# Self-attention with the keys on partitions: scores made turned, maxima from a rough first pass, totals by a ones matmul

## What is computed

```python
def cross_attention(x, ctx, wq, wk, wv, wo, bo):      # self-attention: x and ctx are both layer_norm(x)
    q = jnp.einsum('bne,ef->bnf', x, wq).reshape(B, N, HEADS, DHEAD).transpose(0, 2, 1, 3)
    k = jnp.einsum('bme,ef->bmf', ctx, wk).reshape(B, M, HEADS, DHEAD).transpose(0, 2, 1, 3)
    v = jnp.einsum('bme,ef->bmf', ctx, wv).reshape(B, M, HEADS, DHEAD).transpose(0, 2, 1, 3)
    scores = jnp.einsum('bhnd,bhmd->bhnm', q, k) * SCALE
    attn = jax.nn.softmax(scores, axis=-1)
    out = jnp.einsum('bhnm,bhmd->bhnd', attn, v)
    out = out.transpose(0, 2, 1, 3).reshape(B, N, HEADS * DHEAD)
    return jnp.einsum('bnf,fe->bne', out, wo) + bo
```

## Time and profile before

| | us |
|---|---|
| median of 3 runs | 1040.16 (1039.8 to 1040.65) |
| span of the profiled execution | 1036.7 |
| TensorE busy in it | 981.3 |
| VectorE busy | 690.3 |
| ScalarE busy | 591.5 |
| GpSimd busy | 380.1 |

### The profile page before, as it was taken

How to read it: one execution, slowest core, us unless ns; L and a number is a source line. 1 busy time by engine, 2 the same in 40 slices (tenths; PEclk the granted TensorE clock), 3 DMA queues, 4 the chain that set the end, 5 groups by cost and what they waited for, 6 DMA issues and landing times.

```text
span 1036.7 us, 17534 instructions
## 1 busy us (share of the span) xinstructions
PE 981.3 (95%) x6376; PEld 707.1 (68%) x6376; DVE 690.3 (67%) x1171; ACT 591.5 (57%) x1332; POOL 380.1 (37%) x493
## 2 busy tenths in 40 slices
PE   7999978999999999999999999999989999999998
PEld 4566666666667656667666667666647589999887
DVE  2767646677773776773676773776753889999563
ACT  2666634766763667763667763667753555455442
POOL 2576623434332344342344341343330024444220
PEclk9999999999999999999999999999999999999999
DMA  6400050000000000000000000000000340000000
GB/s 134 94 2 1 1 147 1 1 1 2 1 1 2 1 1 2 1 1 1 2 1 1 1 1 1 2 1 1 2 1 8 101 110 1 1 1 1 2 26 26
DMA packets 25370, 17.64 MB, mean 17 GB/s; under 512 B 8565, under 2 KB 24101, under 8 KB 25285
## 3 DMA queue, kind: packets, MB, share of 16 engines
q1 hardware_dynamic: 25285, 16.52, 6.6%
HBM read 11.26 MB, written 1.31 MB: 12 GB/s over the span
## 4 chain that ended last, share of the span: by engine, by line
PE 64%; DVE 10%; ACT 5%; issue 4%; POOL 1%; DMA 0%; SPq 0%; DVEq 0%; ACTq 0%; POOLq 0%
PE banks L409 13%; PE banks L396 12%; PE banks L382 11%; PE banks L416 4%; ACT sa_probs L499 3%; PE banks L224 3%; PE banks L227 2%; PE banks L226 2%; PE banks L225 2%; PE banks L1641 2%; PE banks L1933 2%; DVE sa_negmax L571 2%; DVE ca_top L1776 2%; DVE ca_probs L1781 1%; PE banks L232 1%
## 5 line engine op out<-in xcount | busy, mean ns | idle before, releaser
L639 POOL TENSOR_SCALAR sa_probs<-sa_probs,sa_inverse 128x512 f32<-128x512 f32 x320 | 217.7, 696 | 372.4 <-DVE sa_inverse L575 372.3
L499 ACT ACTIVATE sa_probs<-banks,sa_negmax 128x512 f32<-128x512 f32 x320 | 215.8, 685 | 163.5 <-DVE sa_negmax L571 163.4
L571 DVE TENSOR_REDUCE sa_negmax<-banks 128x2 f32<-128x1024 f32 x160 | 188.8, 1219 | 12.4 <-PE banks L382 9.7
L396 PEld LDWEIGHTS banks<-ident,sa_probs 128*128 128x128 f32 x1280 | 145.7, 141 | 55.6 <-issue 27.6
L396 PE MATMUL banks<-ident,sa_probs 128*128 128x128 f32 x1280 | 174.0, 277 | 10.0 <-ACT sa_turned L510 5.8
L580 DVE COPY sa_turned<-banks 128x512 f32<-128x512 f32 x160 | 110.2, 689 | 76.3 <-PE banks L396 76.3
L409 PE MATMUL banks<-sa_turned,sa_v 128*64 128x512 f32 x640 | 155.0, 605 | 0.0
L382 PE MATMUL banks<-sa_k_parts,sa_q_parts 64*128 64x512 f32 x960 | 134.9, 412 | 1.9 <-ACT sa_probs L499 1.9
L510 ACT COPY sa_turned<-banks 128x512 f32<-128x512 f32 x160 | 94.3, 590 | 30.6 <-PE banks L396 28.8
L382 PEld LDWEIGHTS banks<-sa_k_parts,sa_q_parts 64*128 64x128 f32 x960 | 85.2, 187 | 31.2 <-issue 14.4
L409 PEld LDWEIGHTS banks<-sa_turned,sa_v 128*64 128x64 f32 x640 | 38.7, 136 | 74.3 <-issue 73.0
(11 more groups left out here) (218 smaller groups left out, 1724.9 us busy)
## 6 DMA issues: line engine op xcount, KB each, us to landing
w_o<-in_L_xattn_wo SPq DMA_DIRECT2D x2, 800.0 KB, 9.2
out<-x SPq DMA_DIRECT2D x4, 320.0 KB, 2.4
w_q_t<-in_L_xattn_wq_t SPq DMA_DIRECT2D x1, 1120.0 KB, 10.4
fold_values<-ca_turned SPq DMA_DIRECT2D x5, 192.5 KB
x<-in_x SPq DMA_DIRECT2D x1, 960.0 KB, 5.8
fold_values<-ca_probs SPq DMA_DIRECT2D x4, 192.5 KB
w_q_t<-in_L_xattn_wq SPq DMA_DIRECT2D x1, 640.0 KB, 6.6
w_o<-in_L_xattn_wk SPq DMA_DIRECT2D x1, 640.0 KB, 10.0
```

Of the source, the lines that this page charges most:

```text
L396: last = pe.transpose(b_turn[e][:, q * P:(q + 1) * P], probs[:, j % 2, e, q, k * P:(k + 1) * P], ident[:])
L499: act.activation(probs[:, j % 2, e, q, :], b_scores[u % 2][:, e, :], ACT.Exp, bias=negmax[:, u % RING, e:e + 1], accum_out=total[:, u % RI ...
L571: dve.tensor_reduce(negmax[:, u % RING, :], b_scores[u % 2], AX_X, ALU.max, negate=True).then_inc(s_max.sem, 1)
L639: pool.tensor_scalar(probs[:, j % 2, e, q, :], probs[:, j % 2, e, q, :], inverse[:, u % RING, e:e + 1], 1.0, ALU.mult, ALU.mult).then_inc( ...
```

## The change

The loop now runs over 40 pairs g = 10 b + j. The scores are made with the keys on partitions (k the stationary operand, q the moving one), so the exponentials come out in the form in which the product with v wants them, and the transposes and their copies are gone. The maximum over keys can't be taken along partitions, so it comes from a first pass: `rough_scores` makes hi·hi alone with queries on partitions, VectorE takes the negated maxima into `negmax` (columns 0 and 64 of 65, the rest zero), `turn_shift` turns them into a row for each head, ScalarE copies the rows into `shift`, and each unit of `scores` gets a fourth product, ones times `shift`, which subtracts the maximum. (Any shift near the maximum gives the same softmax.) ScalarE makes one exponential of 128 x 1024 a unit, without bias or total. GpSimd adds the four units' probabilities (`add`, three additions of 128 x 1024); `totals` multiplies the sum by ones, which spreads each query's total over 64 partitions; VectorE inverts that in four pieces of 128 columns (`invert`), and multiplies `att` by it (`normalize`), after the product with v. The copy of v moves from VectorE to ScalarE. `project_out` works in column halves, and for the first three batches it stands inside the pair with j = 1 of the next batch; so the operands of the norm are doubled (`ln.second`). GpSimd fills the constants at the start. The scores of unit k of a pair, the rough scores of the next pair and the products of the pair ahead alternate in TensorE's order.

```diff

...
-    NU = NPAIR * QT
-    ND = NU // 2
-    LEAD = 2
-    RING = 8
+    NG = B * NPAIR
+    NK = S // P
+    RING = 3
+    V_RING = 2
+    PIECES = 4
+    STATS_AT, HAT_AT, TURN_MAIN, TURN_TAIL, ROUND_AT = 2, 3, 4, 5, 6
...
-        probs = sb("probs", [P, 2, 2, QT, S])
-        turned = sb("turned", [P, 2, 2, S])
+        q_parts = sb("q_parts", [P, RING, 2, S], F32R)
+        k_parts = sb("k_parts", [P, RING, 2, S], F32R)
+        v = sb("v", [P, V_RING, QT, 2 * P])
+        probs = sb("probs", [P, NK, 2, S])
+        sums = sb("sums", [P, 2, 2, S])
         att = sb("att", [P, NPAIR, S])
+        negmax = sb("negmax", [P, 2, QT, HD + 1], F32R)
+        shift = sb("shift", [P, 2, S], F32R)
+        inverse = sb("inverse", [P, S])
+        ones_r = sb("ones_r", [P, P], F32R)
+        ones = sb("ones", [P, HD])
+        ident_r = sb("ident_r", [P, P], F32R)
+        ln.second = (sb("y_hi", [P, S], F32R), sb("y_lo", [P, S], F32R), sb("y_tail", [3 * DT, S], F32R))
...
-        b_scores, b_turn, b_out, b_proj = [banks.pair(0), banks.pair(2)], banks[4:6], banks[6], banks[7]
+        b_keys, b_max = [banks.pair(0), banks.pair(2)], banks.pair(4)
+        b_proj, b_v, b_shift, b_out, b_sum = banks[0], banks[1], banks[4], banks[6], banks[7]
...
+            def rough_scores(g, u, bank):
+                if u == 0:
+                    pe.wait_ge(s_qhi.sem, s_qhi.at(0, g))
+                    pe.wait_ge(s_khi.sem, s_khi.at(0, g))
+                for e in range(2):
+                    last = pe.matmul(bank[:, e, :], q_parts[half(e), g % RING, 0, u * P:(u + 1) * P], k_parts[half(e), g % RING, 0, :],
+                                     start=True, stop=True)
+                last.then_inc(s_rough.sem, 1)
+
+            def next_rough(g, u):
+                pe.wait_ge(s_max.sem, s_max.at(0, unit(g, u) - 1))
+                if u == 0:
+                    pe.wait_ge(s_shift.sem, s_shift.at(0, g - 1))
+                rough_scores(g, u, b_max)
+
+            def turn_shift(g):
+                if g == 0:
+                    pe.wait_ge(s_ident, 1)
+                pe.wait_ge(s_max.sem, s_max.at(0, unit(g, QT - 1)))
+                for i in range(QT):
+                    last = pe.matmul(b_shift[0:HD + 1, i * P:(i + 1) * P], negmax[:, g % 2, i, :], ident_r[:], start=True, stop=True)
+                last.then_inc(s_row.sem, 1)
+
+            def scores(g, k):
+                if k == 0:
+                    pe.wait_ge(s_qlo.sem, s_qlo.at(0, g))
+                    pe.wait_ge(s_klo.sem, s_klo.at(0, min(g + 1, NG - 1)))
+                    pe.wait_ge(s_vsb.sem, s_vsb.at(0, min(g + 1, NG - 1)))
+                    pe.wait_ge(s_shift.sem, s_shift.at(0, g))
...
+                if unit(g, k) >= 2:
+                    pe.wait_ge(s_exp.sem, s_exp.at(0, unit(g, k) - 2))
+                bank = b_keys[k % 2]
+                for i, (a, c) in enumerate(((0, 0), (0, 1), (1, 0))):
                     for e in range(2):
+                        pe.matmul(bank[:, e, :], k_parts[half(e), g % RING, a, k * P:(k + 1) * P], q_parts[half(e), g % RING, c, :],
+                                  start=(i == 0), stop=False)
+                for e in range(2):
+                    last = pe.matmul(bank[:, e, :], ones_r[half(e), :], shift[half(e), g % 2, :], start=False, stop=True)
...
-            def turns(b, u):
-            def pv(b, u):
+            def products(g, k):
+                pe.wait_ge(s_exp.sem, s_exp.at(0, unit(g, k)))
                 if k == 0:
+                    pe.wait_ge(s_vsb.sem, s_vsb.at(0, g | 1))
+                    if g > 0:
+                        pe.wait_ge(s_raw.sem, s_raw.at(0, g - 1))
                 for e in range(2):
+                    c = g % 2 * P + e * HD
+                    last = pe.matmul(b_out[half(e), :], v[:, g // 2 % V_RING, k, c:c + HD], probs[:, k, e, :],
+                                     start=(k == 0), stop=(k == NK - 1))
+                last.then_inc(s_pv.sem, 1)
+
+            def totals(g):
+                pe.wait_ge(s_add.sem, s_add.at(0, (NK - 1) * g + NK - 2))
+                if g > 0:
+                    pe.wait_ge(s_inv.sem, s_inv.at(0, PIECES * g - 1))
+                for e in range(2):
+                    last = pe.matmul(b_sum[half(e), :], ones[:], sums[:, g % 2, e, :], start=True, stop=True)
+                last.then_inc(s_sum.sem, 1)
+
+            def project_out(bank, q, first, end):
+
+                for j in range(first, end):
+                    for e in range(2):
+                        r = q * P + e * HD
+                        last = pe.matmul(bank[half(e), :], att[:, j, r:r + HD], w_o[:, j, :], start=(j == 0), stop=(j == NPAIR - 1))
+                return last
...
+            ln.ready(pe, 0)
+            for g in range(2):
+                project_q(g, b_first[g, "q"])
+                project_k(g, b_first[g, "k"])
+            pe.wait_ge(s_const, 4)
+            rough_scores(0, 0, first_max[0])
+            project_v(0, b_first[0, "v"])
+            pe.wait_ge(s_qlo.sem, s_qlo.at(0, 1))
+            rough_scores(0, 1, first_max[1])
+            project_v(1, b_first[1, "v"])
+            pe.wait_ge(s_klo.sem, s_klo.at(0, 1))
+            rough_scores(0, 2, first_max[2])
+            pe.wait_ge(s_max.sem, s_max.at(0, 0))
+            rough_scores(0, 3, first_max[3])
+            turn_shift(0)
...
+            for g in range(NG):
+                b, j = divmod(g, NPAIR)
+                norm, nb, at = following(b)
+
+                if g + 1 < NG:
+                    next_rough(g + 1, 0)
+                scores(g, 0)
+                scores(g, 1)
+                if g + 1 < NG:
+                    next_rough(g + 1, 1)
+                if j == TURN_MAIN:
+                    norm.turn_main(pe, at, ident, b_v, lambda: pe.wait_ge(s_exp.sem, s_exp.at(0, unit(g, 0))))
+                if j == TURN_TAIL:
+                    norm.turn_tail(pe, at, ident, b_v, lambda: pe.wait_ge(s_exp.sem, s_exp.at(0, unit(g, 0))))
+                if g + 2 < NG:
+                    if j == NPAIR - 2:
+                        ln.ready(pe, b + 1)
+                    pe.wait_ge(s_exp.sem, s_exp.at(0, unit(g, 0)))
+                    project_q(g + 2, b_proj)
+                if g > 0:
+                    totals(g - 1)
+                    products(g - 1, 2)
+                    products(g - 1, 3)
+                if j == 1 and b > 0:
+                    pe.wait_ge(s_att.sem, s_att.at(0, g - 2))
+                    pe.wait_ge(s_exp.sem, s_exp.at(0, unit(g, 1)))
                     for q in range(QT):
+                        last = project_out(b_keys[1][:, q // 2, q % 2 * D:(q % 2 + 1) * D], q, 0, NPAIR)
+                        if q % 2 == 1:
+                            last.then_inc(s_o.sem, 1)
+
+                if g + 1 < NG:
+                    next_rough(g + 1, 2)
+                scores(g, 2)
+                scores(g, 3)
+                if g + 1 < NG:
+                    next_rough(g + 1, 3)
+                if g + 2 < NG:
+                    pe.wait_ge(s_exp.sem, s_exp.at(0, unit(g, 2)))
+                    project_k(g + 2, b_proj)
+                    project_v(g + 2, b_v)
+                if g + 1 < NG:
+                    turn_shift(g + 1)
+                products(g, 0)
+                products(g, 1)
+
+            products(NG - 1, 2)
+            products(NG - 1, 3)
...
+            def exps(g, k):
+                act.wait_ge(s_scores.sem, s_scores.at(0, unit(g, k)))
+                if g > 0:
+                    act.wait_ge(s_pv.sem, s_pv.at(0, unit(g - 1, k)))
+                    act.wait_ge(s_add.sem, s_add.at(0, (NK - 1) * (g - 1) + max(k - 1, 0)))
+                act.activation(probs[:, k, :, :].rearrange("p e q -> p (e q)"), b_keys[k % 2].rearrange("p e q -> p (e q)"), ACT.Exp).then_inc(s_exp.sem, 1)
...
+                exps(g, 0)
+                exps(g, 1)
+                if j == TURN_MAIN:
+                    norm.scale_main(act, at, b_v)
+                if j == TURN_TAIL:
+                    norm.scale_tail(act, at, b_v)
+                if g + 2 < NG:
+                    round_q(g + 2, b_proj)
+                if j == ROUND_AT:
+                    norm.round(act, at, operands_free(nb))
+                if g > 0:
+                    copy_products(g - 1)
+                exps(g, 2)
+                exps(g, 3)
+                if g + 2 < NG:
+                    round_k(g + 2, b_proj)
+                    copy_v(g + 2, b_v)
+                if g + 1 < NG:
+                    copy_shift(g + 1)
...
+            def maxima(g, u, bank):
+                dve.wait_ge(s_rough.sem, s_rough.at(0, unit(g, u)))
+                if g >= 2 and u == 0:
+                    dve.wait_ge(s_row.sem, s_row.at(0, g - 2))
+                to = negmax[:, g % 2, u, 0:HD + 1:HD]
+                dve.tensor_reduce(to, bank, AX_X, ALU.max, negate=True).then_inc(s_max.sem, 1)
+
+            def invert(g, i):
+                if i == 0:
```

(55 more changed lines are left out.)

446 lines of the change are left out of this document (155 added, 291 removed).

## The result

The changed kernel takes 1013.05 us (median, 1012.27 to 1013.34) against 1040.28; the ratio is 0.974, with a 95% interval of 0.9727 to 0.9754. The direction was right, the size was not: I forecast 1032 with a range from 1017, and it is 27 us faster instead of 8.

The account below looks back on a forecast made before the run. TensorE was taken to bound the kernel, VectorE's chain just fitting. Start 171.5, first pair 10.8, 37 pairs 508.8, output projections 35.7, norms 18.4, pair 38 12.2, last 23.8 end self-attention at 781.2, not 789.3: 1032 us, range 1017 to 1053.

Parts of the forecast that it names:

- the price of a plain pair: Self-attention, one head pair without norm step: 13.75 us when nothing waits, set by TensorE, against 13.76 before.
- the hold of the multiplication: VectorE's multiplication of att, two SBUF inputs, beside GpSimd's additions: possibly 1.17 us more, priced as costing the sum nothing.
- The norm steps: Statistics, standardizing and remainder on VectorE between second piece and third maximum: exposed, 3.7 us a batch, 4.6 with eight transposes.
- the gap behind the output projection: TensorE idle, then at clock 0.65, as the next maxima waited for x's update: 7 us of disturbance, all but 0.2 going.
- The out-projection step: Output projection as 40 side-by-side pairs of column halves: 11.7 us against 11.08; three entered the sum at 35.7.
- The pair on TensorE: TensorE's work per head pair: transposes −3.66, added products +2.12, totals +0.94, turning +0.44, net −0.16 us; taken as 13.75.
- The piece of reciprocal: VectorE's inversion of totals, four pieces of 128 columns: extrapolated to 1.01 to 1.22 us each, taken as 1.20.
- rival (b): A reciprocal piece on VectorE is only 1.01 us, giving its chain 0.55 us slack: 1017 to 1025 us; chance 0.18.
- my walk: Step-by-step timing of one pair on TensorE and VectorE: their chains meet twice with about 0.05 us between, pair 13.75.
- rival (a): VectorE's chain, not TensorE, sets the pair and the kernel gets slower: 1040 to 1055 us; chance 0.33.
- The start: Self-attention before the loop: projections to 164.4, VectorE's four maxima to 170.15, turning and copy; loop begins at 171.5 us.
- (c): Column halves of the output projection don't run side by side: 22.2 us each, 1074 in all; chance 0.04.

## Why the prediction was wrong

The step that failed is the price of a plain pair. The prediction took 13.75 us of TensorE's work and nothing for the hold of the multiplication; the runs show 13.14 of work and 0.36 for the hold, 13.50. The two errors go in opposite ways, and that the sum is not further off is luck. The norm steps and the output projection were priced too high as well.

**The bound and the gap: right.** TensorE sets the plain pair, and the gap behind the output projection went whole. The out-projection step was sized 11.9 and took 10.87 (24.37 − 13.50).

**The pair on TensorE: mis-sized, the largest term.** The step gave "−0.16", that is 13.60, and then "I take 13.75". Without a wait it is 13.14 (the kernel with the moved multiplication). Of the 0.61, 0.15 is that rounding up, which no row asked for. The score-shaped matmuls, old and added, were priced 3.18 + 2.12 = 5.30 and take 5.16 (rough products 1.46 with their changes of shape, 16 pairs 3.70): 1.59/6 = 0.265 a side-by-side pair holds, once in six, the longer step at a change of shape (0.33 to 0.43 from start to start at rough products), and the pace inside a run of equal ones is 0.23 (295.89 to 296.12). The turning takes 0.34 instead of 0.44, totals 0.91 instead of 0.94, products with the values 3.69 instead of 3.74, the three projections 3.10 instead of 3.19. That makes 13.20 in the changed kernel, with 0.3 of waiting beside it, and 13.14 in the other, where rough product 1 follows without a gap and takes 0.07 less. Each is small, all go one way, and 0.6 a pair over 37 pairs is 22 us.

**The piece of reciprocal: wrong, 0.95 for 1.20.** The rows allowed 1.01 to 1.22, and I took the upper end by the 2-element row of another stage (0.152) and a small addition for PSUM. The last two rows, 8 to 10 elements, gave 7 ns an element; the chip shows (946 − 217)/118 = 6.2. The repeat count of 8 in the Trainium skill ("VectorE: DVE Perf Modes", the fixed hardware budget), read as eight cycles an element, would give 8.3 as an estimate; the measurement decides against reading it so. So the mechanism of rival (b), given 0.18, was the case, with a piece even shorter than its 1.01 and a time below its 1017: VectorE had 0.27 to 0.43 us to spare at the third maximum, by the way of counting.

**The hold of the multiplication: mechanism right, cost wrong.** The rule was weighed and set at nothing, because with 1.17 more "the next maximum would still be in time for rough 1". It wasn't: in my walk TensorE comes to it 2.5 us behind rough product 0, in the trace it is free after 2.18 (294.87 to 297.05), and the multiplication ends 1.29 behind that start where the walk has 1.15. So TensorE waits 0.3; taking the hold away gave 12.1 us. This is also the wait for `sa_negmax` that was to show rival (a), at the first maximum and by another cause. GpSimd's additions, 2.37 instead of 2.0, lengthen the hold. The Trainium skill ("GPSIMD Engine Reference", Key points) names two SBUF inputs and 2-port modes as what contends. The traces agree for the multiplication, which has two SBUF inputs, and for the statistics, with one, which were not held. Standardizing was held too (2.68 for 1.18), though it reads one tensor; no trace here shows in which mode it runs.

**The norm steps: exposed, but less.** Priced 4.6 a batch; 3.06 in the changed kernel over plain pairs of 13.50, because a pair delayed by a norm step has no held multiplication behind it (pair 7 takes 13.14). Over 13.14, in the kernel with the moved multiplication, they cost 4.1.

**The sum.** From the second to the 38th pair I had 508.8 + 35.7 + 18.4 = 562.9; the trace has 544.1: pairs −9.3 (37 × 0.25), output projections −3.1, norm steps −6.2. The start was 2.2 longer: TensorE waited 2.3 us for the first maxima, and then had a granted clock of 0.50 (1.2 GHz) from 170 to 174 us. The end was 2.1 shorter. Together this is the 18.7 us by which the stage was off. Two smaller errors cancel each other: the rest of the span grew by 1.4, and the 3.5 us between span and time are 1.8 in every run that has both on record, as the profiled execution of the kernel before was faster than its median. (The terms given for the last pair add up to 23.6, not 23.4.) The range failed since it took each bound from one rival at a time: a short piece, a cheap turning and a pair of 13.60 hadn't been put together. As a whole (a) did not occur, and neither did (c): the 40 column-half pairs take 10.96 us (328.55 to 339.51), so they run side by side.

## What to carry to other kernels

Before crediting a large rewrite, ask what its new order removes by accident: here nearly half of the gain can be had by filling the gap behind the output projection, and three moved lines give it to the old kernel too. When GpSimd gets work beside VectorE, read what the one does at the very time at which the other's operations start; a free gap of VectorE is only free for an operation that can be held if GpSimd is quiet in it. Price added matmuls from starts inside a run of equal ones, without the changes of shape, and carry the bounds of all terms together into the range.

## What was new of the hardware

An operation of VectorE that reads two SBUF operands, or the standardizing `tensor_scalar`, does not slow down in proportion beside a running GpSimd addition but all but stops until that addition ends: 1.97 us for 0.69, ending 0.55 behind the addition; 2.68 for 1.18; 2.80 for 0.54. GpSimd's additions have a median of 2.37 us with the hold and without. Where the order is the other way round GpSimd pays, as one case shows: at the end of the stage in the changed kernel a multiplication starts at 738.74, between two additions, and takes 0.69, and the addition that starts at 738.99 takes 2.68. The rests of k (one operand in PSUM, one in SBUF) take their 0.69 beside an addition, and so do maxima and pieces. A reciprocal of 128 elements from PSUM takes 946 ns where one of 10 from SBUF takes 217, 6.2 ns for each further element. An addition of two full 128 x 1024 operands on GpSimd takes 2.37, where the row with a broadcast operand had suggested 2.0.
